# Feed-forward matmuls one unit a pair, and both V groups ahead of both maxima, in a pre-norm attention block on one core

## What is computed

```python
xn = _layernorm(x)
q, k, v = split(xn @ w_qkv)                     # B=2, S=2048, H=16, dh=16
q, k = filter(q), filter(k)                     # a fixed linear map within a head
attn = softmax(q @ k.T / 4)                     # 2048 x 2048 for each of 32 heads of a sequence
a = (attn @ v) @ w_out + b_out
h = square(relu(xn @ W_fc.T))                   # 256 -> 1024
y = h @ W_proj.T                                # 1024 -> 256
# five times: reset = mem > 1; mem = 0.9 * mem + y - reset; spike = mem > 1
out = x + a + sum(spikes) / 5
```

## Time and profile before

| | us |
|---|---|
| median of 3 runs (lowest, highest) | 1985.82 (1983.6, 1986.22) |
| the profiled execution | 1984.17 |
| its span in the trace | 1982.4 |
| PE busy | 1886.5 (95%) |
| DVE busy | 1380.9 (70%) |
| ACT busy | 1091.0 (55%) |
| POOL busy | 708.3 (36%) |

### The profile page before, as it was taken

How to read it: one execution, slowest core, us unless ns; L and a number is a source line. 1 busy time by engine, 2 the same in 40 slices (tenths; PEclk the granted TensorE clock), 3 DMA queues, 4 the chain that set the end, 5 groups by cost and what they waited for, 6 DMA issues and landing times.

```text
span 1982.4 us, 35556 instructions
## 1 busy us (share of the span) xinstructions
PE 1886.5 (95%) x14480; PEld 1063.6 (54%) x14480; DVE 1380.9 (70%) x1659; ACT 1091.0 (55%) x1253; POOL 708.3 (36%) x948
## 2 busy tenths in 40 slices
PE   7889999999999999999999999999999999999998
PEld 4545555555555555555555555555555555555556
DVE  5576777777777777777677777777777777776737
ACT  3225555555555555555555555555555555555562
POOL 1002334444433344444333344443333444443333
PEclk9989999999999999999999999999999999999999
DMA  4660222212102212121012222121122221210104
GB/s 162 220 187 7 39 39 39 38 33 38 25 20 38 39 39 38 33 38 37 16 31 39 38 39 39 33 38 22 24 38 38 39 38 33 39 35 15 33 23 148
DMA packets 46523, 94.58 MB, mean 48 GB/s; under 512 B 10326, under 2 KB 25430, under 8 KB 42266
## 3 DMA queue, kind: packets, MB, share of 16 engines
q1 hardware_dynamic: 46364, 92.35, 21.1%
HBM read 70.80 MB, written 20.99 MB: 46 GB/s over the span
## 4 chain that ended last, share of the span: by engine, by line
PE 72%; DVE 14%; ACT 8%; DMA 2%; issue 2%; SPq 1%; DVEq 0%; ACTq 0%
PE banks L665 21%; PE ring L655 20%; PE ring L645 14%; DVE pmax L869 11%; ACT probs L504 8%; PE banks L724 6%; PE banks L731 6%; DMA qk_scratch<-hid_sb 1%; PE banks L639 1%; PE banks L581 1%; DVE shift L893 1%; SPq L246 1%; PE ring L791 1%; DMA attn<-x 1%; PE ring L572 0%
## 5 line engine op out<-in xcount | busy, mean ns | idle before, releaser
L869 DVE TENSOR_REDUCE pmax<-ring 128x2 f32<-128x1024 f32 x1000 | 1188.6, 1220 | 503.1 <-PE ring L647 503.1
L504 ACT ACTIVATE probs<-ring 128x1024 f32<-128x1024 f32 x1024 | 993.0, 1021 | 751.3 <-PE ring L655 751.3
L655 PE MATMUL ring<-qst,kst 66*128 66x512 f32 x2048 | 616.0, 422 | 2.2 <-ACT probs L504 2.1
L665 PE MATMUL banks<-probs,vst 128*32 128x256 f32 x8192 | 549.9, 386 | 0.1
L655 PEld LDWEIGHTS ring<-qst,kst 66*128 66x128 f32 x2048 | 346.0, 188 | 260.9 <-issue 206.5
L645 PE MATMUL ring<-kst,qst 64*128 64x512 f32 x1000 | 414.9, 465 | 35.6 <-ACT probs L504 21.0
L647 PE MATMUL ring<-kup,qup 64*128 64x512 f32 x1000 | 415.0, 465 | 0.0
L665 PEld LDWEIGHTS banks<-probs,vst 128*32 128x32 f32 x8192 | 214.2, 109 | 252.1 <-issue 162.6
L413 POOL TENSOR_TENSOR hid_sb<-relu_sb 128x512 f32<-128x512 f32 x64 | 66.5, 1039 | 634.2 <-ACT relu_sb L513 634.2
L645 PEld LDWEIGHTS ring<-kst,qst 64*128 64x128 f32 x1000 | 161.4, 184 | 239.6 <-DVE pmax L869 92.5
L418 POOL TENSOR_TENSOR lif<-lif 128x256 f32<-128x256 f32 x32 | 19.6, 612 | 425.9 <-ACT y_sb L521 425.9
(11 more groups left out here) (80 smaller groups left out, 723.3 us busy)
## 6 DMA issues: line engine op xcount, KB each, us to landing
qst<-qk_scratch SPq DMA_DIRECT2D x128, 128.0 KB, 4.0
kst<-qk_scratch SPq DMA_DIRECT2D x64, 256.0 KB, 6.0
qup<-qk_scratch SPq DMA_DIRECT2D x252, 64.0 KB, 5.1
qk_scratch<-probs SPq DMA_DIRECT2D x32, 256.0 KB
kup<-qk_scratch SPq DMA_DIRECT2D x64, 128.0 KB, 6.3
attn<-x SPq DMA_DIRECT2D x8, 512.0 KB, 7.7
qk_scratch<-relu_sb SPq DMA_DIRECT2D x16, 256.0 KB
qk_scratch<-hid_sb SPq DMA_DIRECT2D x16, 256.0 KB
```

The lines of the kernel that those rows point to most:

```text
L504: act.activation(probs[:, s % PS, :], score_slot(g), ACT.Exp, scale=SCALE).then_inc(exp_done, 1)
L655: mm = pe.matmul(score_slot(g)[:, c * BLK:(c + 1) * BLK], kst[b][:, kt * P:(kt + 1) * P], qst[b][:, q:q + BLK], start=True, stop=True)
L665: mm = pe.matmul(po[32 * j:32 * (j + 1), half * D:(half + 1) * D], vst[b][:, kt, :], quarters[:, j], start=(kt == 0), stop=(kt == TB - 1))
L869: dve.tensor_reduce(pmax[:, tile, first:first + 2], unit_slot(g).rearrange("p (c e) -> p c e", c=2), AX, ALU.max).then_inc(mx_taken, 1)
```

## The change

The order in a pair becomes S0, F, S1, V, M0, M1. The wait of S1, of M0 and of M1 stay as they are, each at its matmul. F becomes one unit in each of the 16 pairs: chunks 6 and 7 of `up` at s = 6 and 8, `down` at s = 10 to 24, and chunks 0 to 5 of the *next* tile's `up` at s = 26 to 36. The very first tile's six chunks stand in the three pairs ahead of the passes, two in each. The shift transposes stay at s = 10 and 26, in F, now each with a unit behind it; their output moves to the last quarter of the bank. ScalarE takes `relu_sb` at s = 34 and 10, y at s = 26. GpSimd squares the next tile's first half behind the spiking unit. VectorE does all three instructions of `split_shift` ahead of the reduce of s = 8 and s = 24. The diff, with most unchanged lines left out:

```diff
--- before.py
+++ after.py
@@ -206,9 +206,10 @@
         def use(i, k):
-            return USES * i + 1 + k
-        UP_A, SHIFT_1, UP_B, DOWN, SHIFT_0 = range(USES)
+            return USES * i + 3 + k
+        SHIFT_1, DOWN, SHIFT_0, UP_A, UP_B = range(USES)
+        shift_out = misc[0:16, 3 * P:4 * P]
@@ -402,16 +403,18 @@
...
+            def square(tile, part, k):
+                c = slice(part * FC // 2, (part + 1) * FC // 2)
+                pool.wait_ge(misc_taken, use(tile - 1, k) + 1)
+                pool.tensor_tensor(hid_sb[:, c], relu_sb[:, c], relu_sb[:, c], ALU.mult).then_inc(squared, 1)
+            square(0, 0, UP_A)
             def head(h, b, last=False):
...
                     stage_v(h + b, 1 - b, STEPS * i + PS)
-                for part, k in enumerate((UP_A, UP_B)):
-                    c = slice(part * FC // 2, (part + 1) * FC // 2)
-                    pool.wait_ge(misc_taken, use(i, k) + 1)
-                    pool.tensor_tensor(hid_sb[:, c], relu_sb[:, c], relu_sb[:, c], ALU.mult).then_inc(squared, 1)
+                square(i, 1, UP_B)
@@ -433,6 +436,8 @@
...
                 pool.tensor_copy(counts[:, bass.ds(i, 1), :].rearrange("p a d -> p (a d)"), acc).then_inc(lif_done, 1)
+                if not last:
+                    square(i + 1, 0, UP_A)
@@ -472,7 +477,7 @@
...
                 act.wait_ge(shift_in, 32 * landed)
-                act.activation(shiftT[:, :].bitcast(F32R), misc[0:16, 0:P], ACT.Copy).then_inc(misc_taken, 1)
+                act.activation(shiftT[:, :].bitcast(F32R), shift_out, ACT.Copy).then_inc(misc_taken, 1)
@@ -503,24 +508,27 @@
...
+            def take_up(tile, part, k):
+                act.wait_ge(misc_full, use(tile - 1, k) + 1)
+                act.wait_ge(squared, 2 * tile + part + 1)
+                act.activation(relu_sb[:, part * FC // 2:(part + 1) * FC // 2, :],
+                               misc.rearrange("p (f t) -> p f t", f=FC // 2), ACT.Relu).then_inc(misc_taken, 1)
             def head(h, b, last=False):
...
                 for s in range(FIRST, STEPS + FIRST):
-                    if s in (10, 16):
-                        k, part = (UP_A, 0) if s == 10 else (UP_B, 1)
-                        act.wait_ge(misc_full, use(i, k) + 1)
-                        act.wait_ge(squared, 2 * i + part + 1)
-                        act.activation(relu_sb[:, part * FC // 2:(part + 1) * FC // 2, :],
-                                       misc.rearrange("p (f t) -> p f t", f=FC // 2),
-                                       ACT.Relu).then_inc(misc_taken, 1)
+                    if s == 10:
+                        take_up(i, 1, UP_B)
                     if s == 12:
                         take_shift(use(i, SHIFT_1), 2 * i + 1)
-                    if s == 24:
+                    if s == 26:
                         act.wait_ge(misc_full, use(i, DOWN) + 1)
...
                         take_shift(use(i, SHIFT_0), 2 * i + 2)
+                    if s == 34 and not last:
+                        take_up(i + 1, 0, UP_A)
                     if s < STEPS or not last:
@@ -528,6 +536,8 @@
...
             for s in range(FIRST):
+                if s == 4:
+                    take_up(0, 0, UP_A)
                 exponentials(s, s)
@@ -617,7 +627,7 @@
...
                 pe.wait_ge(lo_done, QB * NB + QK_BANKS)
-                pe.matmul(misc[0:16, 0:P], shift[:], ident[:], start=True, stop=True).then_inc(misc_full, 1)
+                pe.matmul(shift_out, shift[:], ident[:], start=True, stop=True).then_inc(misc_full, 1)
@@ -636,7 +646,7 @@
...
                 pe.wait_ge(misc_taken, u)
-                pe.matmul(misc[0:16, 0:P], shift[:], ident[:], start=True, stop=True).then_inc(misc_full, 1)
+                pe.matmul(shift_out, shift[:], ident[:], start=True, stop=True)
@@ -691,6 +701,8 @@
...
                     scores(g, s % STEPS, sb_)
+                beside()
+                if scored:
                     if g == 0:
@@ -698,7 +710,14 @@
...
                     scores(g + 1, (s + 1) % STEPS, sb_)
-                beside()
+                for v in (s - LAG, s - LAG + 1):
+                    if v >= 0 and (v < STEPS or not last):
+                        if v % TB == 0:
+                            pe.wait_ge(po_taken, 2 * i + v // TB)
+                            pe.wait_ge(vst_ready, i + 1 + v // STEPS)
+                        times_v(STEPS * i + v, v % STEPS, b if v < STEPS else 1 - b)
                 if ahead:
@@ -706,55 +725,61 @@
...
                     maxima(g, (s - LEAD) % UNITS, mb)
-                if ahead:
                     pe.wait_ge(exp_done, g + 3)
...
-                for v in (s - LAG, s - LAG + 1):
-                    if v >= 0 and (v < STEPS or not last):
-                        if v % TB == 0:
-                            pe.wait_ge(po_taken, 2 * i + v // TB)
-                            pe.wait_ge(vst_ready, i + 1 + v // STEPS)
-                        times_v(STEPS * i + v, v % STEPS, b if v < STEPS else 1 - b)
-            def up(f0, tok, last_of):
-                for f in (f0, f0 + 1):
-                    for c in range(KC):
-                        mm = pe.matmul(misc[:, (f % 4) * P:(f % 4 + 1) * P], wfc_sb[:, c, f * P:(f + 1) * P],
-                                       xnT[:, c, bass.ds(tok, P)], start=(c == 0), stop=(c == KC - 1))
-                if last_of:
-                    mm.then_inc(misc_full, 1)
-            def down(f0, last_of):
-                for f in (f0, f0 + 1):
-                    mm = pe.matmul(misc[:, 0:D], hid_sb[:, f, :], wproj_sb[:, f, :],
-                                   start=(f == 0), stop=(f == FC - 1))
-                if last_of:
-                    mm.then_inc(misc_full, 1)
+            def up(tile, f):
+                for c in range(KC):
+                    mm = pe.matmul(misc[:, (f % 4) * P:(f % 4 + 1) * P], wfc_sb[:, c, f * P:(f + 1) * P],
+                                   xnT[:, c, tile * P:(tile + 1) * P], start=(c == 0), stop=(c == KC - 1))
+                return mm
+            def down(f):
+                return pe.matmul(misc[:, 0:D], hid_sb[:, f, :], wproj_sb[:, f, :],
+                                 start=(f == 0), stop=(f == FC - 1))
...
-                    if s in (6, 8):
-                        if s == 6:
-                            pe.wait_ge(misc_taken, use(i, UP_A))
-                        up(s - 6, i * P, s == 8)
+                    if s == 6:
+                        up(i, 6)
+                    if s == 8:
+                        up(i, 7).then_inc(misc_full, 1)
                     if s == 10:
                         transpose_shift(2 * i + 1, use(i, SHIFT_1))
-                    if s in (12, 14):
-                        if s == 12:
-                            pe.wait_ge(misc_taken, use(i, UP_B))
-                        up(s - 8, i * P, s == 14)
-                    if s in (16, 18, 20, 22):
-                        if s == 16:
-                            pe.wait_ge(misc_taken, use(i, DOWN))
-                        pe.wait_ge(squared, 2 * i + 2 + (1 if s < 20 else 2))
-                        down(s - 16, s == 22)
-                    if s == 26 and not last:
+                        pe.wait_ge(squared, 2 * i + 3)
+                        down(0).then_inc(misc_full, 1)
+                    if s == 12:
+                        pe.wait_ge(misc_taken, use(i, DOWN))
+                        down(1)
+                    if s in (14, 16):
+                        down((s - 10) // 2)
+                    if s == 18:
+                        pe.wait_ge(squared, 2 * i + 4)
+                        down(4)
+                    if s in (20, 22):
+                        down((s - 10) // 2)
+                    if s == 24:
+                        down(7).then_inc(misc_full, 1)
+                    if last:
+                        return
+                    if s == 26:
                         transpose_shift(2 * i + 2, use(i, SHIFT_0))
+                        up(i + 1, 0).then_inc(misc_full, 1)
+                    if s == 28:
+                        pe.wait_ge(misc_taken, use(i, UP_A))
+                        up(i + 1, 1)
+                    if s == 30:
+                        up(i + 1, 2)
+                    if s == 32:
+                        up(i + 1, 3).then_inc(misc_full, 1)
+                    if s == 34:
+                        pe.wait_ge(misc_taken, use(i, UP_B))
+                        up(i + 1, 4)
+                    if s == 36:
+                        up(i + 1, 5)
@@ -765,8 +790,22 @@
...
             pe.wait_ge(xnt_copied, NB + 2)
+            def first_up(s):
+                if s == 0:
+                    pe.wait_ge(misc_taken, use(-1, UP_A))
+                    up(0, 0)
+                    up(0, 1)
+                if s == 2:
+                    up(0, 2)
+                    up(0, 3).then_inc(misc_full, 1)
+                if s == 4:
+                    pe.wait_ge(misc_taken, use(-1, UP_B))
```

(15 more changed lines are left out.)

## The result

The changed kernel takes 2041.91 us (median of 4 runs, 2040.88 to 2042.38), the kernel before 1984.71 on the same chips: 1.0292 times as long, 95% interval 1.0273 to 1.031. The prediction was 1985 in a range from 1950 to 2022: wrong, by 57 us.

The account below looks back on a forecast made before the run. Before, eight pairs of a pass were bound by TensorE, eight by the exponential's circle, 56.21 us. The new circle gives 14 x 3.48 + 2 x 3.75 = 56.2; 1984.17 + 0 + 1.4 - 0.9, median 1985 us, range 1950 to 2022.

Parts of the forecast that it names:

- What bounds the kernel before: Old pairs: without units the exponential's circle binds at 3.28 us (reduce circle 2.96), with two units TensorE's issue at 3.65.
- The new circle, 3.48: M0, its reduce, next S1, V, next M0: 0.55 + 1.22 + 0.05 + 0.66 + 1.00 = 3.48 us a pair.
- The price of V -> M0: Step from V's issue to M0's, seen in no row: taken as 1.00 us, like V to S0.
- the low end without a price: V to M0 without the cost of changing tile shape: 3.39 us a pair, 1940 us; chance 0.07.
- One reading in the sum: TensorE's two score matmuls ahead of V: 0.34 + 0.23, the 0.34 read as 1.12 less three paces.
- Shift pairs, 3.75: Pairs s = 10 and 26: shift transposes add 0.53 us of issue to 3.22, giving 3.75; range 3.48 to 3.95.
- What costs nothing, and its cover: VectorE's output steps at s = 18 and 34, and other engines' work, fit idle time; the transpose in 1.12 us.
- a cover of 0.08: With the division between the reduces, the second reduce ends at 3.35 us and M0 wants it at 3.48.
- last sign of being wrong: Listed sign against the forecast: M0 waiting for the second reduce in the pairs with the division.
- Rival 3: V to M0's tile-shape change dearer, in every pair's circle: at twice the price 3.57 us a pair, 2030 us; chance 0.18.
- rival 1: Reduce done when TensorE reaches S1, so TensorE's issue binds: 3.22 us a pair, 1873 us; chance 0.10.
- The small terms: Ends of the kernel: first three pairs about 2.1 us more, thirteen following bring back 0.7; last pass +0.4 and -1.3.

Follow-up runs that it names:

- run 2: Changed kernel with only V put back behind both maxima (S0, F, S1, M0, M1, V), one unit in each pair: 1909.57 us, 0.9628 of the kernel before.
- run 3: Changed kernel's spread feed-forward work in the order of the kernel before (S0, S1, F, M0, M1, V): 1911.74 us, 0.9634 of the kernel before.
- run 1: Changed kernel with VectorE's transpose of V's output one step earlier, at s = 17 and 33: 1984.45 us, 1.001 of the kernel before.
- run 10: run 1 with the reduce of each even step over half its columns, leaving out half of those scores: 1877.22 us, 0.9473 of the kernel before.
- run 6: Changed kernel with 11 of 16 feed-forward units left out in every pass but the first: 2147.49 us, 1.0834 of the kernel before.
- Run 11: run 2 with VectorE's division one step later, plus shift transposes moved right ahead of V and their unit behind V: 1908.7 us, 0.9629 of the kernel before.
- run 9: run 3 with split_shift back where the kernel before has it: 1931.66 us, 0.9749 of the kernel before.
- Run 5: Kernel before with the changed order and the early split_shift, feed-forward units still in lumps: 2109.73 us, 1.0636 of the kernel before.

## Why the prediction was wrong, point by point

- *What bounds the kernel before*, two circles and TensorE's issue: held. Runs 2 and 3 took the lumps away and left 3.27.
- *The new circle, 3.48*: held to 0.01 in every ordinary pair; run 1 has 3.48 to 3.49 in all 14, run 10 shortened it by its reduce, run 6 showed that TensorE's work is not in it. *The price of V -> M0*, the step without a row: 1.00 as taken. The Trainium skill's rule ("TensorEngine Tiling (Array Packing)", section Key Properties: a changed tiling mode drains TensorE) agrees: the low end without a price, 3.39 a pair, did not come. Run 11 shows the other side: two transposes of 16 columns right ahead of V's 32-column tiles take 0.23. One reading in the sum is off without effect: 1.12 less three paces of 0.23 is 0.43 and includes the change to V; the 0.34 from S0's first matmul to its second is right by the earlier trace rows.
- *Shift pairs, 3.75*: held at 3.75; without the early `split_shift` 4.23 in the old order (run 9).
- *What costs nothing, and its cover*: **here is the step that failed.** I costed VectorE's output steps by VectorE's own idle time (1.12, the transpose fits) and asked who was late for the *reduces*. I didn't ask who waits for the *transpose*. The first V of each half of a pass does (`po_taken`). While V stood last in the pair it came after the next maxima were issued, and the transpose had ended 1.05 us before or more; with V moved ahead of M0 it is wanted 2.48 us after the M0 of the pair before, and V can go only at 3.31. The term taken at 0 was 0.83 x 62 = 51 us. An instruction that is moved takes its own waits with it, and this one had a wait in each 16 steps. Run 1, which only does the transpose sooner, takes V's wait away and brings 1984.45.
- The same paragraph gave *the division* a cover of 0.08 with the delay of one row. Beside GpSimd it takes 0.57 to 0.62 at s = 34, in 31 of 32 passes, and 0.31 less 0.08 is the 0.23 at s = 4: 7 us more. Together 58, the miss. The prediction's own last sign of being wrong, M0 waiting for the second reduce in a pair with the division, did come there.
- *The rivals*: none was this. Rival 3 named the right side and nearly the right time (2030) by a mechanism that is absent. The 3.22 of rival 1 is a real bound, as run 10 shows, but behind the circle.
- *The small terms*: the first three pairs were to take 2.1 us more and took 14.41 us before and after, so they are no part of the miss.

What the change is made of, by runs: spreading alone 1931.7 against about 1981, -50; the early `split_shift` -20; V ahead of the maxima +75 (run 2 to run 1) and +57 for transpose and division (run 1 to the changed kernel). The 75 are a net: the circle costs 14 x 0.21 x 31 = 91, and 16 go off since run 2 loses 0.44 and 0.07 a pass by the division at s = 4 and 20 and run 1 doesn't. With -2 for F between the scores (run 3 to run 2) the steps sum to 60 us over the 1981 on those chips; the result's own kernel before took 1985.

## What to carry to other kernels

Before a group of instructions is moved ahead in a queue, list every wait inside it, the rare ones too, and ask for each when its releaser ends in the new order; a wait once in 16 steps is missed in the picture of an ordinary step. Where two engines pass slots to and fro, anything put between the wait for a slot and the next use of the other engine lengthens their circle by its whole length. An engine's idle time covers an instruction only if nobody waits for its end before that time is over.

## What the runs showed of the hardware that was not expected

- **VectorE behind GpSimd.** VectorE's `tensor_tensor` of two SBUF inputs takes 0.29 us alone. Started 0.15 to 0.38 us into a GpSimd `tensor_tensor` of 0.73 it took 0.50 to 0.72 and ended 0.15 behind it; that is nearly every pass of the changed kernel and of runs 2 and 3, and two passes of the kernel before. Started 0.14 to 0.18 into a `tensor_scalar` of 0.85 it took 0.36 to 0.40 and ended 0.31 ahead of that one's end (8 passes of run 9, the last pass of eight other kernels). Started 0.59 or more into the first, or 0.32 or more into the second, it took 0.29. By these rows, as an estimate, it is held up until 0.59 behind the start of the `tensor_tensor` (0.88 less 0.29) and 0.25 behind that of the `tensor_scalar` (0.54 less 0.29). The Trainium skill ("SBUF — State Buffer", section SBUF: two separate sides) has a VectorE instruction with two SBUF inputs and a GpSimd instruction that reads SBUF exclude each other, by a lock on a shared port pair, for the whole instruction. That a wait exists agrees in both cases; its length agrees nearly for the `tensor_tensor` and not for the `tensor_scalar`, and the measurement decides.
- **Less work, slower.** Run 6 left out 11 units of 16 and lost 105 us: its granted clock fell to half 47 times, always in a pair with V's wait for the transpose, and 0.59 was granted over the 4 us shown. Run 5, whose units stand in lumps, has 19 such falls, which cost a pass some 2.4 us each. The changed kernel crosses the same waits without a fall. Which of several like waits brings a fall isn't told by these runs: some passes of the same program have it and some don't.
